# Cross-attention kernel, second attention: where VectorE takes the row sums and in what order TensorE issues a unit's score products

## What is computed

```python
xn, ln = layernorm(x, ...), layernorm(latents, ...)       # x is the context (77), latents the 1024 tokens
q = (ln @ Wq).reshape(b, m, h, d).transpose(0, 2, 1, 3)   # 16 heads of 64
kv = jnp.concatenate([xn @ Wkv, ln @ Wkv], axis=1)        # 77 + 1024 keys
qn, kn = rmsnorm(q, qn_g) * d ** -0.5, rmsnorm(k, kn_g)
sim = jnp.where(mask, jnp.einsum('bhid,bhjd->bhij', qn, kn), max_neg)
out = jnp.einsum('bhij,bhjd->bhid', softmax(sim), v)
return out.transpose(0, 2, 1, 3).reshape(b, m, h * d) @ Wout + bout
```

## Time and profile before

| | before |
|---|---|
| median of 3 runs | 2242.23 us |
| profiled execution: its time / its span | 2242.01 us / 2240.2 us |
| busy: PE, DVE, ACT, POOL | 1945.1 (87%), 1274.5 (57%), 1017.9 (45%), 605.9 (27%) |
| mean granted clock of TensorE | 0.937 |
| second attention, 636.0 to 1841.1 us: PE busy | 1121.37 of 1205.10 us |

### The profile page before, as it was taken

How to read it: one execution, slowest core, us unless ns; L and a number is a source line. 1 busy time by engine, 2 the same in 40 slices (tenths; PEclk the granted TensorE clock), 3 DMA queues, 4 the chain that set the end, 5 groups by cost and what they waited for, 6 DMA issues and landing times. The chain is left out here.

```text
span 2240.2 us, 40112 instructions
## 1 busy us (share of the span) xinstructions
PE 1945.1 (87%) x13656; PEld 1669.3 (75%) x13657; DVE 1274.5 (57%) x2963; ACT 1017.9 (45%) x1747; POOL 605.9 (27%) x555
## 2 busy tenths in 40 slices
PE   4888948999479999998999999999999994799994
PEld 2568948999367777777877877777778774699994
DVE  4273065676756666766676666667766776122223
ACT  2543315554245455544554555455545551344441
POOL 2300012333251432343143314323432300122220
PEclk9998958999689999999999999999999995899997
DMA  5502162111322211211321122122212207311113
GB/s 193 168 35 94 38 246 94 47 49 42 112 56 67 60 31 45 67 41 28 67 67 38 30 67 55 32 50 67 51 30 56 60 1 266 120 38 34 36 37 125
DMA packets 93663, 159.24 MB, mean 71 GB/s; under 512 B 22385, under 2 KB 54831, under 8 KB 91707
## 3 DMA queue, kind: packets, MB, share of 16 engines
q1 hardware_dynamic: 82875, 134.32, 21.3%
q0 software_dynamic: 8320, 20.65, 3.1%
q10 hardware_dynamic: 2304, 2.10, 0.3%
HBM read 71.57 MB, written 32.41 MB: 46 GB/s over the span
## 5 line engine op out<-in xcount | busy, mean ns | idle before, releaser
L1823 ACT ACTIVATE a_prob<-a_slot,a_npeak 128x1024 f32<-128x1024 f32 x256 | 285.7, 1116 | 307.1 <-DVE a_npeak L1882 306.8
L1880 DVE TENSOR_REDUCE a_part_peak<-a_slot 128x1 f32<-128x512 f32 (+1 forms) x512 | 349.2, 724 | 13.3 <-PE a_slot L1689 13.3
L1689 PE MATMUL a_slot<-a_KHL,a_QHL 128*128 128x512 f32 (+1 forms) x1536 | 317.5, 356 | 1.7 <-ACT a_latT L1257 1.7
L1689 PEld LDWEIGHTS a_slot<-a_KHL,a_QHL 128*128 128x128 f32 x1536 | 260.2, 189 | 47.6 <-ACT a_latT L1257 2.1
L1639 PE MATMUL a_side<-a_W,a_latT 128*128 128x128 f32 x1536 | 217.5, 294 | 80.3 <-DVE a_KT L1890 62.8
L1639 PEld LDWEIGHTS a_side<-a_W,a_latT 128*128 128x128 f32 x1536 | 192.9, 202 | 114.5 <-DVE a_KT L1890 77.2
L1714 PE MATMUL a_po<-a_probT,a_V 128*64 128x256 f32 (+1 forms) x2304 | 276.8, 385 | 0.0
L1698 PE MATMUL a_slot<-ident,a_prob 128*128 128x128 f32 x2048 | 276.6, 280 | 0.0
L1835 ACT ACTIVATE a_probT<-a_slot 128x640 f32<-128x640 f32 x256 | 180.5, 705 | 197.6 <-PE a_slot L1698 196.2
L1698 PEld LDWEIGHTS a_slot<-ident,a_prob 128*128 128x128 f32 x2048 | 244.4, 146 | 9.2 <-issue 1.2
L1903 DVE COPY a_probT<-a_slot 128x512 f32<-128x512 f32 x256 | 176.9, 691 | 90.8 <-PE a_slot L1698 89.3
(11 more groups left out here) (319 smaller groups left out, 2984.4 us busy)
## 6 DMA issues: line engine op xcount, KB each, us to landing
a_KHL<-a_KT SPq DMA_DIRECT2D x128, 256.0 KB, 4.1
a_QHL<-a_QT SPq DMA_DIRECT2D x128, 128.0 KB, 2.4
m_up<-_L_ffn_gate_up_proj_dram SPq DMA_DIRECT2D x8, 1024.0 KB, 9.7
m_up<-in_L_ffn_W_dram SPq DMA_DIRECT2D x8, 1024.0 KB, 9.0
m_down<-in_L_ffn_W_dram SPq DMA_DIRECT2D x8, 1024.0 KB, 13.2
a_prob_dram<-a0p_zeros SPq DMA_DIRECT2D x4, 1632.0 KB
a_dist_dram<-a_dist SPq DMA_DIRECT2D x4, 1632.0 KB, 8.2
a_band_prob<-a_prob_dram SPq DMA_DIRECT2D x4, 1632.0 KB, 6.8
```

What stands on the lines that cost most here:

```text
L1689: ins = t_.matmul(out[:, lo:hi], q, KHL[:, pair.parity, h, part, lo:hi], start=part == 0, stop=part == 1)
L1823: a_.activation(prob[:, u % 2, 0:SEQ], slot[u % 2][:, 0:SEQ], ACT.Exp, bias=bias, accum_out=latent_sum[:, u % 2:u % 2 + 1])
L1880: v.tensor_reduce(part[:, i:i + 1], slot[u % 2][:, lo:hi], AX.X, ALU.max).then_inc(part_peaked, 1)
```

## The change

In the PE program the three products of a unit are issued in another order, with the two short matmuls in the middle. In the DVE program of an iteration `row_sum(u)` goes to its head, `row_sum(u + 1)` behind `normalise` where there is one, and `invert` goes behind the two peaks. Nothing is added or taken away.

```diff
-                for lo, hi in ((0, BANK), (BANK, SEQ), (SEQ, W2)):
+                for lo, hi in ((0, BANK), (SEQ, W2), (BANK, SEQ)):
...
                 for u in range(0, UNITS, 2):
                     one_before, two_before = group_before(pair, u, 1), group_before(pair, u, 2)
+                    row_sum(pair, u)
                     if u % 4 == 0 and two_before[0]:
                         normalise(*two_before)
+                    row_sum(pair, u + 1)
                     if u % 4 == 2 and one_before[0]:
                         dve.wait_ge(turned, (pair.g * UNITS + u) * 3 + 1)
                         copy_sums(*one_before)
...
                     copy_first(pair, u + 1)
-                    row_sum(pair, u)
-                    row_sum(pair, u + 1)
-                    if u % 4 == 2:
-                        invert(pair, u // 4)
                     for k in range(2):
                         nxt = ahead(pair, u + k, 2)
                         if nxt[0]:
                             peak(*nxt)
+                    if u % 4 == 2:
+                        invert(pair, u // 4)
```

## The result

The changed kernel takes **2151.37 us** (median of 4 runs, 2147.54 to 2157.47), before 2242.35 us (4 runs): a ratio of **0.9594**, with a 95% interval of 0.9567 to 0.962. The forecast was 2154 in a range of 2142 to 2193.

What follows compares the result with a forecast made beforehand. PE was taken as nearly the bound of the second attention (busy 1121.37 of 1205.10 us), losing time to waits and a lowered clock: 2242.0 - 68 (waits) - 21 (clock) = 2153, stated as 2154 us, range 2142 to 2193.

Steps and rivals of the forecast that it cites:

- The wait at u = 6: PE's wait for DVE's `KT` at iteration 6 of a pair: 3.2 of 3.44 us gained, 0.2 left.
- u = 8: PE's wait for `KT` at iteration 8 of a pair: 0.47 of 0.56 us goes, 0.1 left.
- u = 12: PE's wait for `qgam` at iteration 12: `Qtb` copied about 1.1 us earlier, so the 0.6 us wait goes.
- Sum of the waits: PE's waits for `KT` and `qgam` over fifteen pairs: 62.8 + 9.6 - 15 x 0.3 = 68 us gained.
- The clock: Matmuls made longer by a clock of 0.50 behind waits for `KT`: 21 of 23 us back, bounds 0 and 23.
- What the moved sums stand ahead of: DVE's copies and PE's next scores behind the moved sums: the sums fit between, nothing taken as lost.
- the named margins: At u = 6 the sum ends at 1205.0, L1592 starts at 1205.4; L1603 is 0.5 us from a sum at u = 14.
- the first rival: Long POOL instruction (L1592 or L1603) holds a sum, copies 1 to 2 us late, PE waits at scores: 2188 us, chance 0.14.
- Short products in the middle: PE's new order of a unit's three score products: 0 gained; bounds 6 us lost and 25 gained.
- the bound of +6: Long matmul at the end finishing up to 0.2 us later at u = 6 and u = 8: 6 us lost.
- The second rival: POOL's power and one instruction behind it hold the sums at u = 6 and u = 10: 2225 us, chance 0.07.

Runs made afterwards that it cites:

- experiment one: Changed kernel with the old order of the score products, so the DVE part of the change alone: 2148.04 us, ratio 0.9581.
- experiment three: Kernel before with the row sums moved, `invert` left ahead of the peaks, old order of products: 2150.04 us, ratio 0.9589.
- five: Kernel before, DVE order unchanged, with POOL's squares, folds and scalings working on one tile each: 2178.61 us, ratio 0.971.
- four: Kernel before with `invert` moved behind the peaks, sums left behind the copies, old order of products: 2202.67 us, ratio 0.9827.
- experiment two: Kernel before with only the new order of the score products, DVE as before: 2239.88 us, ratio 0.9987.
- experiment six: Changed kernel with POOL's squares, folds and scalings shortened to one tile each: 2149.24 us, against 2151.37.
- eight: Changed kernel with the old order of products and two more POOL squares between bound and power of the queries: 2158.96 us, ratio 0.9615.

## Why the prediction was right

- **The wait at u = 6** (3.2 of 3.44 us gained): all of it went, in all fifteen pairs. Two steps were off by a little and against each other. The first product was taken at 0.62 us behind the scores' start and is there at 0.74; the wide copy, taken as perhaps held for 0.9, slipped in before a fold and took 0.30. The exponentials started 2.42 us behind the scores (predicted 2.21), the subtraction 1.94 behind them, as the row of before gave it.
- **u = 8** (0.1 left): 0.25 is left, for the same 0.12, the 0.08 that the new order puts before the second maximum, and the rounding. That makes 3.7 us; the other 2.8 of the 6.6 are the two waits ahead of the first pair.
- **u = 12** (0.6 gone): gone.
- **Sum of the waits**: 68 predicted, 69.6 us of idleness measured, and part of this closeness is luck. The prediction took all 62.8 + 9.6 as waits of the fifteen pairs; 3.6 of it (1.4 twice, and 0.8 for `qgam`) lie ahead of them and stayed. For it stood in that PE also waited at u = 10, at L1675, 4.1 us in all, which went and which the sum did not have. The waits that it named gave 65 us, the unnamed one 4.
- **The clock**: 21 of 23 predicted. PE's busy time in the fifteen pairs fell from 1071.14 to 1047.40 in experiment one, which has the old order of products and no fall of the clock in them: so 23.7 us were to be had. In the changed kernel it fell by 19.5 to 1051.60; the other 4.2 are the new order and one fall. Where the waits at u = 6 are gone (after, experiments one and three) or under 0.7 us (five), the clock never falls behind them; where they are some 2.0 us long (four), it falls behind five of fifteen, and where they are 3.4 us and more (before, and two), behind eleven and eight, each time within 1.6 us of the wait's end. It is not the length of this wait alone: the seventh, eighth, twelfth and thirteenth pair of before have the same 3.4 to 3.5 us and keep a clock of 1.00. Why is open. The other falls come behind the edge of a loop, where PE stood for 1.4 to 2.1 us (one after, one each in experiments four, five and six, two in eight), or stand at the head of the first pair.
- **What the moved sums stand ahead of**: nothing, as forecast, and the named margins were real. L1592 missed the sum of unit 7 by 0.7 us. L1603 did hold that of unit 15, as the first rival feared, and the copies were still through 0.3 us before PE came for them. Not seen in the prediction: the sums of units 4 and 5 came under L1580 and its folds, the longest for 2.23 us. That this costs nothing is experiment six's result, not the prediction's.
- **Short products in the middle** (0, bounds -25 and +6): no difference in two comparisons. The records give a loss of some 3 us, inside the bounds, so the 0 was a little too good. Most of it is not the late maximum that the bound of +6 stood for, but busy time of PE itself in every pair.
- **The second rival**, a power that holds the sums, is out: 48 sums started and ended within a power after the change, and all took 0.29 to 0.30 us; 12 more had started at most 0.14 us before the power and took 0.30. The Trainium skill (SBUF — State Buffer, Who interferes with whom) has the two exclude each other for the whole of an instruction. With L1580, L1592, L1603 and the folds the traces agree; with the power on 16 or 18 columns they do not, and the measurement decides.

The forecast lay 2.6 us above the median, within the spread of the runs. The mechanism was the one predicted; that the number came out so close owes something to small errors which cancelled.

## What to carry to other kernels

Before a cheap instruction is called hidden, look at what it stands ahead of on its engine: 0.3 us sums stood between PE's scores and the maxima, and only there were they dear. Where one engine is busy for nearly all of a stage, as PE was here, add up its waits in that stage and the excess of its busy time over its best stretch at full clock; the two together are what a reordering can give back, and here they gave 89 of the 94 us between the two profiled runs. Count only waits that lie inside the stage, and all of them, the small ones too. An instruction that is held while another engine works is better moved to where nobody waits for it than shortened, since it may be held there as well, and free of charge.

## What the runs showed of the hardware that was not expected

- A DVE instruction with two SBUF inputs is held by a long POOL instruction on wide tiles (1.70 us for 0.30), gets in between two of them, and is not held at all by a power on 18 columns of 3.25 us. The hold ends with the POOL instruction, to within 0.1 us.
- `invert`'s wide copy took 1.15 us when it came during a fold, 2.0 us when it came 0.05 us behind the start of L1580 (experiment three), and 0.30 us when a fold started 0.04 us behind it (1164.61 in the changed kernel): in these cases the one that started first went first.
- The granted clock fell behind waits of PE for `KT` of 3.4 us in eleven pairs of fifteen (eight in experiment two), behind waits of 2.0 us in five of fifteen, and behind waits of 0.7 us and less in none. It also fell behind the edge of a loop, where PE stood for 1.4 to 2.1 us.
- PE's matmuls are not evenly spaced. Behind short ones (78 columns, or a transpose) the second long matmul starts 0.32 us after the first, the others 0.23 us. Moving the short ones from the end to the middle of a unit therefore moves such a gap and removes none.
